# One core, a long convolution and a low-rank expert FFN: where one tile's loads, row statistics and token statistics stand in the FFN loop

## The reference

```python
x = x + attn(layernorm(x))      # x is [8, 4096, 512] float32
x = x + ffn(layernorm(x))       # adds to the first 4096 tokens of the flat [b*l, d] only

def attn(x):                    # a long convolution, one kernel per channel, plus x * omega
    p, a = sigmoid(delta), sigmoid(alpha);  q = 1 - p * a
    k = einsum('dnl,dn->dl', p * beta * exp(t * log(q)), gamma / 4)      # 16 states a channel
    return irfft(rfft(x, 2l) * rfft(k, 2l))[:l] + x * omega

def ffn(x):                     # 4096 tokens, 8 experts of rank 64, each token goes to 2 of them
    for e in range(8):
        h = gelu(x @ w1A[e].T @ w1B[e]);   y_e = h @ w2A[e].T @ w2B[e]
    return sum over the 2 experts of a token: weight * y_e
```

## Time and profile before

| | |
|---|---|
| median of three runs | 1070.18 us |
| the profiled execution: its own time, its span | 1070.18 us, 1068.0 us |
| busy: PE, DVE, ACT, POOL | 869.4, 816.4, 761.4, 571.5 us |
| mean granted TensorE clock | 0.94 of full speed |
| FFN stage in that trace | about 380 to 790 us |

### The profile page before, as it was taken

How to read it: one execution, slowest core, us unless ns; L and a number is a source line. 1 busy time by engine, 2 the same in 40 slices (tenths; PEclk the granted TensorE clock), 3 DMA queues, 4 the chain that set the end, 5 groups by cost and what they waited for, 6 DMA issues and landing times.

```text
span 1068.0 us, 31991 instructions
## 1 busy us (share of the span) xinstructions
PE 869.4 (81%) x11186; PEld 730.9 (68%) x11186; DVE 816.4 (76%) x1350; ACT 761.4 (71%) x1124; POOL 571.5 (54%) x641
## 2 busy tenths in 40 slices
PE   2770588887868969999999999997878889786981
PEld 1550477776757758888888888886757777675771
DVE  7988899987969834577777777775689998797891
ACT  3882599997969756566665665664459999696990
POOL 5444788867857232666666656655553333332330
PEclk9995699998989979999999999999989999898996
DMA  8999899999999979999999999899669999999977
GB/s 300 351 400 385 211 264 209 271 266 295 308 279 285 327 182 309 257 293 318 286 312 259 242 268 244 246 256 240 174 157 268 226 252 281 287 296 300 295 159 158
DMA packets 390529, 286.11 MB, mean 268 GB/s; under 512 B 124784, under 2 KB 338434, under 8 KB 389948
## 3 DMA queue, kind: packets, MB, share of 16 engines
q1 hardware_dynamic: 345980, 211.67, 72.6%
q0 software_dynamic: 17952, 34.42, 14.6%
q10 hardware_dynamic: 26528, 39.14, 10.4%
HBM read 195.57 MB, written 98.77 MB: 276 GB/s over the span
## 4 chain that ended last, share of the span: by engine, by line
PE 31%; issue 17%; ACT 15%; DVE 14%; DMA 13%; POOL 3%; SPq 2%; DVEq 1%; ACTq 1%; POOLq 0%
PE ps L1688 8%; DMA xb<-L_attn_x 6%; PE ps L1714 6%; ACT wb L1032 6%; DVE xb L1364 4%; ACT wb L1038 4%; PE ps L1562 4%; PE ps L1575 3%; PE ps L1587 3%; DMA wide<-y_d,slot_g 3%; ACT carry L1008 3%; DVE wb L1182 2%; PE ps L1650 2%; PE ps L1663 2%; DVE state L1380 2%
## 5 line engine op out<-in xcount | busy, mean ns | idle before, releaser
L1575 PE MATMUL ps<-xn,wb 128*128 128x128 f32 x2048 | 273.0, 288 | 0.0
L1575 PEld LDWEIGHTS ps<-xn,wb 128*128 128x128 f32 x2048 | 248.0, 198 | 17.0 <-issue 2.3
L625 POOL TENSOR_TENSOR cen<-xb,mean 128x512 f32<-128x512 f32 x128 | 142.8, 1119 | 217.0 <-DVE state L1380 144.2
L1353 DVE TENSOR_TENSOR xn<-cen,rstd 128x1024 f32<-128x1024 f32 x128 | 177.1, 1384 | 44.9 <-POOL cen L625 36.1
L1140 ACT ACTIVATE cen<-ps 128x1024 f32<-128x1024 f32 x110 | 109.2, 1023 | 101.6 <-PE ps L1688 64.7
L1562 PE MATMUL ps<-xn,near 128*32 128x128 f32 x2048 | 87.5, 291 | 113.0 <-DVE xn L1353 67.9
L1364 DVE TENSOR_TENSOR xb<-xb,ps 128x1024 f32 (+1 forms) x128 | 152.7, 1193 | 7.6 <-PE ps L1587 7.6
L1031 ACT ACTIVATE wb<-wide 32x1024 f32<-32x1024 f32 x126 | 144.5, 1147 | 15.4 <-DMA wide<-taps_d 12.9
L1562 PEld LDWEIGHTS ps<-xn,near 128*32 128x32 f32 x2048 | 52.6, 113 | 137.2 <-issue 72.1
L1688 PE MATMUL ps<-carry,wb 64*128 64x256 f32 x1024 | 126.8, 388 | 7.7 <-DVE carry L1426 4.6
L1688 PEld LDWEIGHTS ps<-carry,wb 64*128 64x128 f32 x1024 | 99.4, 190 | 37.1 <-issue 18.5
(11 more groups left out here) (211 smaller groups left out, 1311.4 us busy)
## 6 DMA issues: line engine op xcount, KB each, us to landing
xb<-L_attn_x SPq DMA_DIRECT2D x160, 512.0 KB, 7.4
out<-xb SPq DMA_DIRECT2D x72, 512.0 KB, 6.4
xb<-L_attn_x ACTq DMA_DIRECT2D x128, 256.0 KB, 5.8
out<-xb SPq DMA_DIRECT2D x88, 256.0 KB, 4.7
wb<-L_ffn_w_B SPq DMA_DIRECT2D x78, 256.0 KB
wide<-taps_d SPq DMA_DIRECT2D x63, 256.0 KB, 5.8
dk<-decay_d SPq DMA_DIRECT2D x63, 128.0 KB, 5.6
out<-y_d SPq DMA_DIRECT2D x4, 1536.0 KB, 11.6
```

Source lines behind the costliest of these rows:

```text
L625: pool.tensor_tensor(cen[:, k, 0:QB // 2].rearrange("p b r d -> p r b d"), unit_view(pool, g, i, k)[:, :, 0:UC // 2] .rearrange("p r (b d) ...
L1353: dve.tensor_tensor(xn[:, k].rearrange("p (b d) r -> p b d r", d=2), cen[:, k].rearrange("p b r d -> p b d r"), rstd[:, g * P:(g + 1) * P] ...
L1575: ins = pe.matmul(ps[:, QB * k + b, d * P:(d + 1) * P], wb[:, h, k * QB + b, d, :], xn[:, k, 2 * b + d, :], start=(b > 0 and d == 0), stop ...
```

## The change

Three functions change place; no operation is added or taken away, except that one `deviation` of the prologue now runs at the start of tile 0.

- DVE: `stage_out(q)` now stands ahead of all row statistics, both halves of these follow together, then `rank_in_half(q + 1)`, and `token_stats(q + 2)` comes last.
- POOL: `deviation(q + 1)` stands at the start of tile q instead of `deviation(q + 2)` near its end.
- ACT: all four loads of the next tile's row groups are issued at the end of a tile, none after `stage_up`.

```diff
@@ POOL, tile(q, m, ...) @@
                 k = m % 2
+                if is_in(q, NQ - 1):
+                    deviation(q + 1, 1 - k)
                 if first:
                     gather(2, 0)
...
                     gather(q + 3, 1 - k, None if isinstance(q, int) else (m + 3) % 4)
-                if is_in(q, NQ - 2):
-                    deviation(q + 2, k)
...
             deviation(0, 0)
-            deviation(1, 1)
@@ ACT @@
-            def rows2(q, i0):
-
-                for i in range(i0, i0 + 2):
-                    load2((q - ROW0) * LR2 + i, i, (q - ROW0) * 2 + i // 2)
...
                     stage_up(q + 1)
-                if not isinstance(q, int) or ROW0 <= q < ROW0 + TT:
-                    rows2(q, LR2 // 2)
...
                 if not isinstance(q, int) or ROW0 <= q + 1 < ROW0 + TT:
-                    rows2(q + 1, 0)
+                    for i in range(LR2):
+                        load2((q + 1 - ROW0) * LR2 + i, i, (q + 1 - ROW0) * 2 + i // 2)
@@ DVE, tile(q, m, ...) @@
                         normal(q + 1, 1 - k, h)
-                if rows:
-                    rows2(q, 0)
-                if is_in(q, NQ - 2):
-                    token_stats(q + 2, k)
                 if first:
                     dve.wait_ge(s_w2b, 32)
                 stage_out(q, e)
                 if rows:
+                    rows2(q, 0)
                     rows2(q, LR2 // 2)
                 if is_in(q, NQ - 1):
                     rank_in_half(q + 1)
+                if is_in(q, NQ - 2):
+                    token_stats(q + 2, k)
```

## The result

The changed kernel takes 1083.0 us (median of four runs, 1077.36 to 1085.74), the kernel before, beside it, 1069.27 us (1064.97 to 1073.61). The ratio is 1.0115, 95% interval 1.0065 to 1.0166: 12 to 14 us slower, outside my range. The profiled execution took 1085.2 us, span 1083.0.

What follows compares the result with a forecast made beforehand. It took POOL's chain of scatters to set the end of the FFN stage, with PE running ahead. From 1070.18 us, pair tiles 0, chain +0.7, ACT 0 and single tiles +1.0 gave 1072 us, range 1065 to 1080.

Steps and rivals of the forecast that it cites:

- What bounds: FFN stage: POOL's chain of scatters, 10.34 us a tile, sets the end; PE runs ahead at 10.20 and waits in single tiles.
- Step 1: DVE's new order in pair tiles: `rank_in_half` no longer waits behind token statistics, so PE's 4.74 us of idling could go.
- Step 2: DVE's later `rank_out` stalls PE's `widen` 0.15 us a tile, bounds 0 and 1.0; pair tiles gain 0.8 us, counted as 0.
- Step 3: POOL's scatters stand behind the later deviation: chain delayed once, not per tile, by 0.7 us, between 0 and 2.15.
- Step 4: ACT's second pair of row loads, issued ahead of `stage_up`, costs 0 and brings loads no sooner.
- Step 5: Single tiles: `rank_in_half`'s wait goes, but tile 38's deviation comes late behind a scatter; +1.0 us, between 0 and 3.0.
- the slower one: Path from `rank` to `widen` exceeds 3.57 us; at 0.45 us a tile 7.3 us more, 1079; chance 0.19.
- The faster rival: Scatter chain doesn't hold the end, or shortens with loads in one block: 7 us gained, 1063; chance 0.15.
- The third, longer issues: POOL's scatters, moved to where DVE copies, issue 0.3 us longer in ten early tiles: 3 us, 1075; chance 0.06.

Runs made afterwards that it cites:

- x3: Kernel before, with each accumulating scatter moving only 128 of 512 columns, to other places: ratio 0.988, 1057.7 us.
- x4: Changed kernel, with each accumulating scatter moving only 128 of 512 columns, to other places: ratio 0.9948, 1067.0 us.
- x1: Changed kernel with ACT's row loads split again as before the change, where the kernel before takes 1072 us: ratio 1.008.
- c2: Changed kernel, unchanged, run again as a control on the same chip as others: ratio 1.0119 to the kernel before.
- e9: Changed kernel with DVE's copy `rank_out` ahead of the reading of the expert's number: ratio 1.0125 to the kernel before.
- e7: e6 with only POOL's deviation made to wait for DVE's copy `rank_out`: ratio 1.0048 to the kernel before.
- e8: e6 with four unused `bn_stats` put behind `rank_in_half` on DVE, so that only `rank_out` is late: ratio 1.0091 to the kernel before.
- e6: Changed kernel with `token_stats` ahead of `rank_in_half` again, everything else as changed: ratio 0.9998 to the kernel before.
- e1: Kernel before with only ACT's four row loads issued in one block, on the slower kind of chip: ratio 1.0003.
- e5: Changed kernel with POOL's part undone, the deviation of tile q+2 at the end of tile q again: ratio 1.0155 to the kernel before.
- e2: Changed kernel with ACT's row loads split again, on the slower kind of chip: ratio 1.0158 to the kernel before, 1096 us.
- e4: Changed kernel with `rank_out` ahead of the reading of the expert's number, on the slower kind of chip: ratio 1.0085 to the kernel before.
- y1: e6 with tile 3's weights issued early and ACT's row loads split, on the slower kind of chip: ratio 0.9997 to the kernel before.
- y2: Changed kernel with tile 3's weights issued early and ACT's row loads split, on the slower kind of chip: ratio 1.0107 to the kernel before.
- e3: Kernel before with `token_stats` behind `rank_in_half` and POOL's deviation moved with it, on the slower kind of chip: ratio 1.0156, 1095 us.

## Why the prediction was wrong, by its steps

What bounds: right as far as it went. A shorter chain is worth 15 us (x3). But I took the chain for the only thing that sets the end, and every loss of PE in front of it for free. It is not: 7 to 9 us of the change's cost remain with a short chain.

Step 1, right in its mechanism: the wait for `rank_in_half` went from the pair tiles, the waits for loads fell to 18.7 us, and none of the 4.74 us were kept.

Step 2, right in mechanism and, without the chain's disturbance, in size: 0.15 us a tile predicted; x4 and x1 have (275.64 - 27 x 10.05) / 27 = 0.16 and 0.18. In the changed kernel the pair tiles took 10.56 us (c2: 10.36) instead of my 10.20. This is the step that failed: "as good as nothing", and the 0 in the sum because "the chain is waited for". The late copy and the late deviation don't hide behind the chain. Taking the copy's lateness away from widen alone gives nothing back (e9), and each costs alone (e7 0.5%, e8 0.9%); only with the statistics back in front of `rank_in_half` is the cost gone (e6).

Step 3 was mis-sized. I wrote +0.7 once, bounds 0 and 2.15. The chain's second scatter started 7.0 us later: 2.04 from the deviation (0.25 to 2.29 into the tile, almost my upper bound), and 4.97 because tile 4 itself was late. My earliest place, 3.3 us into a tile, was too late by the 1.3 us of idle time that I carried over from tile 10: at 448.37 the scatter follows the deviation at once. I had not asked what PE does when it comes early to tile 3. And the scatters were not 10.34 but 10.63 us apart (c2: 10.40), the condition under which I had called the forecast wrong.

Step 4: 0 was right with the statistics in their old place (e1, e6). With the late ones the block may cost up to 0.4% (x1 against c2), not shown.

Step 5: +1.0 predicted with bounds 0 and 3; T31 to the second half is 63.81 + 11.86 against 59.06 + 14.65, +1.96. The size is near by luck, because the named cause pays itself back: tile 38 does start late behind its deviation (8.22 us behind tile 37, before 6.24), but DVE's closing operations are then shorter, and with the deviation back in its place (e5) nothing came back. Nor is the short end the deviation's alone: e1, which leaves it in place, has 11.82 us there too. What stands in the single tiles is the wait for the normalised tokens, of which step 5 only said that they come no earlier, and the clock that falls behind it.

The sum: +5.27 before tile 4, +8.97 in the pair tiles, +1.96 behind, -0.3 at the stage's start is 15.9 in the profiled pair (790.91 to 806.81 at the second half), where I had 0, 0.7 and 1.0. The rival nearest to the truth was the slower one (1079, chance 0.19). Its condition, 0.45 us a tile at widen, was met on the slower kind of chip (e2 against e1: 11.14 - 10.66 = 0.48), and there the pair tiles hold most of the 1.6% (302.6 us against 288.8). The faster rival fell: with the block of loads the landings did not get shorter beyond what one kernel varies by (7.7 and 7.4 us against 7.4 and 7.5), and the block alone gains nothing (e1). The third, longer issues, fell too: scatters took 1.67 us to issue at 448.37 and 513.99.

The Trainium skill, "DMA: Bandwidth & Descriptors", section "Issuing engines are not separate DMA queues", says that transfers of different issuers share the same engines. Tile 3 of the first pair would fit it: its weights, issued by SP, landed 2.4 us later while POOL's gathers came 2 us sooner. That the gathers are the cause is not shown, and e9, with tile 2 as early and tile 3 at 431.50, speaks against it.

## What to carry to other kernels

When an operation is moved behind the last hand-over of a loop body, price the next hand-over with everything that now stands in front of it, reading of registers and the turn of the loop included, and don't book its stall as hidden because another chain is slower: here two nearly equal chains each cost something, and together about the sum (e7, e8, c2). Judge such a stall by the length of iterations, not by the sum of labelled waits. And ask where an engine that becomes early runs into a transfer that lands no earlier than before: the idle time can take the clock with it.

## What the runs showed of the hardware

The same kernel runs in two ways on different chips. Where before took 1071 us, DVE started `rank_in_half` 1.09 us behind the start of `rank`, whenever it was free. Where before took 1078 to 1082 us it was 2.1 us or a little more (e1 to e4, y1, y2), up to the end of the loop and 1.09 us again behind it, with a gap of 0.2 to 0.4 us in the `down` matmuls that follow. e2, PE, then DVE (e3):

```profile
608.22 1.04 PE L1661 MATMUL ps<-xn,xb 128*64 128x128 f32 x16
609.10 0.82 PE L1712 MATMUL ps<-dk,xn 128*64 128x128 f32 x10
610.16 0.49 PE L1712 MATMUL ps<-dk,xn 128*64 128x128 f32 x5 [0.25 <-issue]
```
```profile
609.81 0.29 DVE L1423 COPY carry<-ps 128x128 f32<-128x128 f32 x1 [3.01 <-PE ps L1662]
```

e3's `rank` began at 607.68. PEclk was 1.00. A pair tile took 10.7 us there with the statistics in their old place (e1), and the late copy cost about three times as much (0.48 us a tile, against 0.16 in x4 and 0.18 in x1). I have no cause for it. Whoever compares kernels whose hand-overs are this tight needs the kernel before on the same chip.

The time from a landing to the next scatter was the same in all four profiles of the two kernels, about 1.0 us in nearly every link (0.97 at the median in each). It doesn't explain why executions of one kernel differ by 1%; that stays open.
